# A norm taken one slot later on VectorE, behind the context's low half, in the projections of a cross-attention and expert kernel

## The reference

```python
q = rms_norm(linear(ln(x), q_w, q_b), norm_q_w)             # 16 heads of 32
k, v = rms_norm(linear(ctx[257:], k_w, k_b), norm_k_w), linear(ctx[257:], v_w, v_b)
k_img, v_img = the same of ctx[:257] with weights of its own
x = x + linear(attention(q, k, v) + attention(q, k_img, v_img), o_w, o_b)
x = x + moe(ln(x)) + shared_ffn(ln(x))                      # 32 experts, top 4 of 3 groups
```

## Time and profile before

| | |
|---|---|
| median of 3 runs | 1255.86 us (1254.3 to 1257.92) |
| profiled execution | 1257.99 us, span 1256.2 us |
| TensorE (PE) busy | 1162.2 us, 93% of the span |
| VectorE (DVE) busy | 827.6 us, 66% |
| ScalarE (ACT) busy | 649.6 us, 52% |
| GpSimd (POOL) busy | 186.4 us, 15% |
| granted TensorE clock, mean | 0.986 |

### The profile page before, as it was taken

One profiled execution on the slowest core, in us unless ns is written; L12 is line 12 of the kernel. 1 busy time (PEld: TensorE's weight loads), 2 busy tenths in 40 slices (PEclk: granted clock), 3 DMA queues, 4 the chain that ended last, 5 costly groups with the idle time before them and its releaser, 6 DMA issues. The chain is left out here.

```text
span 1256.2 us, 20731 instructions
## 1 busy us (share of the span) xinstructions
PE 1162.2 (93%) x8484; PEld 417.4 (33%) x8484; DVE 827.6 (66%) x1035; ACT 649.6 (52%) x917; POOL 186.4 (15%) x299
## 2 busy tenths in 40 slices
PE   4988999999899999889999989999899999998996
PEld 2432222344222234322224432222354434333332
DVE  5663888987588898757889875998668952122221
ACT  4446899344699934379983447997131121111221
POOL 0210000033000013300001330000120001333442
PEclk9999999999999999999999999999899999999999
DMA  8643000348400045830003584011733317999842
GB/s 301 155 93 68 2 2 10 98 98 191 92 2 2 10 109 107 186 76 2 2 10 109 121 190 142 2 35 55 282 140 118 117 55 276 354 300 296 250 69 28
DMA packets 139768, 143.02 MB, mean 114 GB/s; under 512 B 107920, under 2 KB 108176, under 8 KB 134416
## 3 DMA queue, kind: packets, MB, share of 16 engines
q1 hardware_dynamic: 134544, 130.78, 35.1%
q0 software_dynamic: 5120, 10.82, 4.7%
HBM read 95.67 MB, written 20.73 MB: 93 GB/s over the span
## 5 line engine op out<-in xcount | busy, mean ns | idle before, releaser
L642 ACT ACTIVATE work<-ps 128x1024 f32<-128x1024 f32 (+1 forms) x416 | 403.0, 1021 | 42.8 <-PE ps L1093 39.0
L1099 PE MATMUL ps<-work,vals 128*32 128x512 f32 (+2 forms) x1664 | 221.9, 606 | 0.9 <-ACT work L642 0.6
L952 PE MATMUL ps<-wts,work 128*128 128x512 f16 x864 | 197.3, 384 | 15.1 <-DVE work L691 15.1
L1093 PE MATMUL ps<-quer,keys 32*128 32x512 f16 x2496 | 172.5, 379 | 21.4 <-ACT work L642 6.8
L863 DVE TENSOR_TENSOR work<-work 128x2048 f32<-128x2048 f32 x64 | 146.6, 2291 | 6.0
L863 DVE TENSOR_TENSOR attn<-attn,work 128x2048 f32<-128x2048 f32 x62 | 142.0, 2290 | 5.9 <-DVE attn L863 0.5
L952 PE MATMUL ps<-wts,hl 128*128 128x512 f16 x480 | 116.4, 396 | 21.6 <-DVE hl L691 12.7
L952 PEld LDWEIGHTS ps<-wts,work 128*128 128x128 f16 x864 | 84.0, 99 | 127.1 <-issue 29.0
L1902 PE MATMUL ps<-wring,xgt 128*80 128x512 f32 x256 | 114.9, 592 | 0.0
L721 DVE SCALAR_TENSOR_TENSOR work<-work,small,vec 128x512 f32<-128x512 f32 (+1 forms) x72 | 65.6, 912 | 68.2 <-POOL small L484 68.1
L1093 PEld LDWEIGHTS ps<-quer,keys 32*128 32x128 f16 x2496 | 46.4, 92 | 191.1 <-ACT work L642 163.8
(11 more groups left out here) (213 smaller groups left out, 1329.4 us busy)
## 6 DMA issues: line engine op xcount, KB each, us to landing
wring<-in_wx SPq DMA_DIRECT2D x32, 1536.0 KB, 9.0
raw<-in_ctx SPq DMA_DIRECT2D x52, 256.0 KB, 3.0
work<-in_x SPq DMA_DIRECT2D x4, 1024.0 KB, 5.4
table<-nums SPq DMA_DIRECT2D x16, 256.0 KB, 2.5
work<-in_x SPq DMA_DIRECT2D x12, 256.0 KB, 4.5
x<-work SPq DMA_DIRECT2D x12, 256.0 KB, 2.5
x2t_rows<-nums SPq DMA_DIRECT2D x12, 256.0 KB, 2.5
x2t<-x2t_rows SPq DMA_DIRECT2D x3, 1024.0 KB, 9.0
```

What stands on the lines that cost most here:

```text
L642: act.activation(prob[0:rows, s % PROBS, 2 * half:2 * half + 2, :], ps[0:rows, 2 * pair:2 * pair + 2, :], ACT.Exp, scale=SCALE).then_inc(a ...
L952: mm = pe.matmul(out, lhs(a, c)[:, cols], wts[:, w, z, c * D:(c + 1) * D], start=(k == 0), stop=(k == len(steps) - 1))
L1093: mm = pe.matmul(ps[:, 2 * pair + h % 2, :], k[h * HD:(h + 1) * HD, :], q[h * HD:(h + 1) * HD, :], start=(e == 0), stop=(e == len(terms) - 1))
L1099: return pe.matmul(ps[h * HD:(h + 1) * HD, NUM, :], vals[a:z, ORDER[n], g * P + h * HD:g * P + (h + 1) * HD], prob[a:z, s % PROBS, h, :], ...
```

## The change

On VectorE, `key_norm` of slot i moves from the end of slot i into slot i+1, behind `ctx_low` of that slot. `key_low` of slot i moves from there to just ahead of `key_raw` of slot i+1, behind the small work. The norm and the low half of slot 16 stand together at the end of the phase. The two weight low halves of batch 0 thus come ahead of the norms of their slots. No other engine's program changes.

```diff
                     if i + 1 in KV_AT and i != (0 if b > 0 else 1):
                         ctx_low(bb, KV_AT[i + 1])
                     if i >= 1:
-                        key_low(bb, i - 1)
+                        key_norm(bb, i - 1)
                     if b == 0 and i == 0:
                         weight_low(p, WK)
                     if b > 0 and i in NORM_SLOT:
@@
                         x_normed(bb, (i - 4) // 2)
                     if i in (5, 7, 9, 11):
                         x_low(bb, (i - 5) // 2)
+                    if i >= 1:
+                        key_low(bb, i - 1)
                     if bb == 0:
                         if i == 0:
                             dve.wait_ge(s_vi, 32)
@@
                     if b > 0 and i - 1 in O_SLOT:
                         out_rows(q, O_SLOT.index(i - 1))
                         out_stats(q, O_SLOT.index(i - 1))
-                    key_norm(bb, i)
                     if b == 0 and i == 4:
                         weight_low(p, WQ)
                     if bb == 0 and i == 7:
@@
                         dve.wait_ge(s_const, 5)
+                key_norm(bb, SLOTS - 1)
                 key_low(bb, SLOTS - 1)
```

## The result

The changed kernel has a median of 1254.28 us over 22 runs, the kernel before 1257.79 over 22 runs beside them. The ratio is 0.9976 with a 95% interval of 0.9966 to 0.9986: 3.0 us faster (1.8 to 4.3; the two medians lie 3.5 apart). That is inside the 0.3% that I called the same, and inside the range, but it is a gain that the interval keeps apart from nothing, where the sum said +0.3 us. The profiled execution took 1256.36 us around a span of 1254.6; the span before was 1256.2.

The account below looks back on a forecast made before the run. The prediction took TensorE to bound the projections' front part and VectorE's chain their tail. Its terms, -0.6 us in batch 0 and +0.3 in each of three others, made +0.3, giving 1256.2 us, range 1252.3 to 1260.5.

Parts of the forecast that it names:

- VectorE's chain decides, TensorE's waits are not the gain: Projection tails: VectorE's chain is re-cut and not shortened, 1256.2 us, own range 1253.5 to 1258.5; chance 0.72.
- The wait ahead of the first scores: TensorE's wait for the raw rows (L708) before the attention's first scores grows to about 2 us from 0.5.
- The sign that TensorE's waits for L691 would fall to less than half: TensorE's waits for VectorE's context low halves, 15.1 + 12.7 us before, would drop below half.
- Parts (a) to (d) of the chain: Per slot: context half earlier; norm later, 0.23 us worse; up to 0.78 us small work hidden; without context half, only hiding.
- the choice for slots 7 and 11: Context half delays GpSimd's bias addition, then norm and output scale: +0.74 and +0.79 us; near +0.15 each if they pass freely.
- that sign: In slots 7 and 11 GpSimd's bias addition starts later after the raw rows, at 2.9 us instead of 2.32.
- The weight slots: Batch 0, slots 4 and 7: the norm comes after the weight low half, costing +0.68 and +1.0 us.
- the small losses: Batch 0, slots 1, 11, 13 and 14 lose 0.24 us each.
- The second rival: Projection tails: collisions go away and TensorE's clock stays up, giving 1249 us; chance 0.10.
- The third rival: Attention start: TensorE idles 2 us before the first scores and its clock falls, 1261.3 us if in batches 1 to 3; chance 0.13.
- The fourth rival: Moved waits on GpSimd all fall dear: +0.9 us in each later batch, +0.3 in batch 0, 1258.9 us; chance 0.05.

Follow-up runs that it names:

- the doubled products: Changed kernel with TensorE making the key product of slots 13 and 15 twice into the same bank; 1255.02 us, ratio 0.9976 to the kernel before.
- the norm's half alone: Kernel before with the norm moved behind the next slot's context low half and the key's low half following at once; 1274.71 us, ratio 1.0127.
- the low half alone: Kernel before with only the key's low half moved behind the small work, the norm staying at the end of its slot; 1250.39 us, ratio 0.994.
- the low half back in two slots: Kernel with only the low half moved, but in slots 8 and 12 put back in front of out_norm; 1250.66 us, ratio 0.9936 to the kernel before.
- the bias moved: Changed kernel with GpSimd adding the output bias after the raw rows, ahead of the key's scale; 1253.1 us, ratio 0.996 to the kernel before.

## Why the prediction was off, point by point

**VectorE's chain decides, TensorE's waits are not the gain:** right, shown by the doubled products (nothing lost) and by the norm's half alone (16 us lost with the context as early). The wait ahead of the first scores grew to 1.7 us (2 predicted). The sign that TensorE's waits for L691 would fall to less than half did not come (27.8 to 23.6 us over the whole kernel).

**Parts (a) to (d) of the chain:** right. The timeline of slots 13 and 14 in the changed kernel:

```profile
310.66 0.68 DVE L708 SCALAR_TENSOR_TENSOR work<-ps,vec 128x512 f32<-128x512 f32 x1
...
313.15 0.69 DVE L691 TENSOR_TENSOR work<-raw,work 128x512 f16<-128x512 f32 x1 [1.82 <-ACT work L549]
313.76 0.75 DVE L721 SCALAR_TENSOR_TENSOR work<-work,small,vec 128x512 f32<-128x512 f32 x1
...
315.80 0.68 DVE L708 SCALAR_TENSOR_TENSOR work<-ps,vec 128x512 f32<-128x512 f32 x1
...
317.78 0.69 DVE L691 TENSOR_TENSOR hl<-raw,hl 128x512 f16<-128x512 f32 x1 [1.29 <-ACT hl L549]
318.39 0.74 DVE L721 SCALAR_TENSOR_TENSOR work<-work,small,vec 128x512 f32<-128x512 f32 x1
319.17 0.62 ACT L563 CAST work<-work 128x512 f16<-128x512 f32 x1 [0.93 <-DVE work L721]
319.82 0.69 DVE L727 TENSOR_TENSOR work<-work 128x512 f16<-128x512 f32 x1 [0.68 <-ACT work L563]
320.43 0.68 DVE L708 SCALAR_TENSOR_TENSOR work<-ps,vec 128x512 f32<-128x512 f32 x1
```

The context half comes 2.49 and 1.98 us after the raw rows (2.52 and 2.01 predicted), slot 14 lasts 4.63 (4.67). Against the earlier trace rows the wait has moved from the norm to the context half, and in slot 14 a wait of 0.68 stands bare ahead of the low half.

**The term that failed is the choice for slots 7 and 11, +0.74 and +0.79: they measured +0.39 and +0.37.** The timeline of slot 11, as in the earlier trace rows:

```profile
298.88 0.68 DVE L708 SCALAR_TENSOR_TENSOR work<-ps,vec 128x512 f32<-128x512 f32 x1
...
301.02 0.66 DVE L691 TENSOR_TENSOR work<-raw,work 128x512 f16<-128x512 f32 x1
301.19 1.61 POOL L509 TENSOR_TENSOR work<-work,vec 128x512 f32<-128x512 f32 x1
301.59 1.76 DVE L721 SCALAR_TENSOR_TENSOR work<-work,small,vec 128x512 f32<-128x512 f32 x1
...
303.49 0.55 POOL L503 TENSOR_TENSOR small<-small 128x1 f32<-128x1 f32 x1
304.07 0.55 DVE L772 TENSOR_SCALAR nums<-work,small 128x512 f32<-128x512 f32 x1 [0.72 <-POOL small L503]
...
305.13 0.69 DVE L708 SCALAR_TENSOR_TENSOR work<-ps,vec 128x512 f32<-128x512 f32 x1
```

The collision came, with both pairs: the addition lasts 1.61 instead of 1.26 under the context half, the norm 1.76 behind the addition. But I let the addition start only when the context half was done, at 2.9 us after the raw rows, and end at 4.16. It started at 2.31, as before (so that sign did not come), 0.17 into the context half's 0.66, and ended at 3.92: it paid 0.35 and not 0.58. Then GpSimd's scales, which I let follow so that the raw rows came at 6.67, were done for an out_norm at 5.19 and raw rows at 6.25. In the old order L503 takes 0.88 beside the context half, as the kernel with the low half alone still shows; here it takes 0.55. I charged the queue behind the collision at the durations of the old order, whose own collisions the move takes away.

Each half of the change alone makes slot 11 0.35 us dearer (6.23): with the norm's half it is the collision, which ends the norm 0.35 later; with the low half it is out_norm's wait, which the run with the low half back in two slots took away (5.88). Together they make 6.25, not 6.6. The two costs run side by side: of the 0.35 that the addition loses, 0.33 comes back in L503 (0.55 instead of 0.88).

The sum was +0.3 us, and the slots of the profile, as added up below, make -3.2: 3.5 apart. Slots 7 and 11 came out 0.35 + 0.42 cheaper in each of three batches, 2.3 us. Another 0.8 is 0.04 to 0.07 in each of slots 5, 6, 8, 13 and 14, three times, and the last 0.4 is batch 0. From the raw rows of slot 1 to those of slot 16 that batch lasts 79.04 instead of 80.02 us: -0.98, where -0.6 was summed. The weight slots cost +0.66 and +0.98 as said (+0.68, +1.0), slots 6, 8 and 10 gave 0.77, 0.79 and 0.60; the small losses were 0.19 to 0.21 and not 0.24 each, and slots 2, 3, 5 and 9 gave 1.24 and not 1.07. In this one profile part of the gain is hidden, because slot 0 of batch 0 lasted 9.28 instead of 8.46: ScalarE waited 4.20 us instead of 3.38 for the load of context tile 2. That wait ended at 20.53, and the first instruction that the change moves, the norm of slot 0, starts at 25.82, so the change did not make it. The slot lasted 8.46 to 10.02 us over the eight kernels; why the load varies, no run isolates. Without it the slots make -0.98 - 0.74 - 0.73 - 0.72 = -3.2 us, close to the measured 3.0.

**The second rival:** a part of it came. The clock stayed up in the tails (1.00 against 0.83 at 310 to 320), but that gave next to no time, since 5.2 us more of TensorE work per tail cost none. Only where the fall ran on into the first scores, in batch 3 of the kernel before, did the exponentials behind the first come 0.3 later. The collisions were cheaper, and that did give time.

**The third rival** did not come in the profile of the changed kernel, but what it feared is in the record. From the raw rows of slot 16 to those of the next batch it takes 120.8 to 121.2 us, and 122.5 where the clock falls early in the attention, as it did in batch 0 of this profile and of the one before. In batches 1 to 3 it fell three times with the norm's half alone (0.50 in 342 to 344, the lower of its two levels of 1.2 and 2.4 GHz), twice with the bias moved, once with the doubled products and once with the low half alone, each time for 1.6 us; in the other profiles never. That is 6 of 12 attentions where the norm is moved and 1 of 12 where it is not. What brings it on stays open. With the norm's half alone TensorE has no wait ahead of the first scores of batch 1; in 340 to 342 it was busy for 0.52 of 2 us, and in 330 to 332 of the changed kernel, where the clock stayed up, for 0.53. How often it fell in the executions behind the median was not measured, so how far it moved the median is not shown.

**The fourth rival** did not come: slots 8 and 12 measured +0.03 and +0.05.

The Trainium skill's page "SBUF — State Buffer", section "SBUF: two separate sides", has the operation that starts first go through and the other blocked for all of it. These rows agree on the winner: the context half kept its 0.66, the addition behind it did not keep its 1.26. The loser paid less than the whole rest: the addition 0.35 where 0.49 of the context half was left, the norm 1.01 where 1.21 of the addition was left.

## What to carry to other kernels

Take the chain of one period from the trace (here raw rows to raw rows) and ask of each operation whether it stands in the shadow of another engine's work; an edit that feeds the next engine sooner can lengthen that chain, while its plainer half carries the gain, as here. When an operation moves, those that it used to collide with get their own time back, so sum the queue behind it at undisturbed durations, and do not add two costs that can run side by side. Whether a wait of the next engine matters at all is tested cheaply by doubling that engine's work there.

## What the runs showed of the hardware

A VectorE operation on two SBUF operands and a GpSimd addition on SBUF hardly share time: 0.75 us became 1.74 to 1.76 in every kernel where the addition was under way, and the addition took 1.61 instead of 1.26 where VectorE was first. With the addition placed beside output rows and statistics, it took 1.27 to 1.28 us and they 0.68 to 0.70, as elsewhere. The one-column scale on GpSimd (L503) took 0.55 us alone and 0.87 to 0.88 beside such a VectorE operation, and a one-column operation of 0.19 us (L481) took 0.73. Out_norm and the norm waited for these short operations.
